# Cross-attention and mixture-of-experts layers: TensorE leaves out repeated semaphore waits, and value products wait once a batch

## The reference

```python
def _L0_xattn_ref(x, ctx, Wq, bq, Wkv, bkv, Wproj, bproj, gq, gk):
    q = (x @ Wq + bq).reshape(B, S, H, HD)
    q = rms_norm(q, gq).transpose(0, 2, 1, 3)
    kv = (ctx @ Wkv + bkv).reshape(B, Sc, 2, H, HD)
    k = rms_norm(kv[:, :, 0], gk).transpose(0, 2, 1, 3)
    v = kv[:, :, 1].transpose(0, 2, 1, 3)
    ...
    scores = jnp.einsum('bhsd,bhtd->bhst', q, k) * scale
    attn = jax.nn.softmax(scores, axis=-1)
    out = jnp.einsum('bhst,bhtd->bhsd', attn, v)
    ...
    return out @ Wproj + bproj
...
x = x + _L0_xattn_ref(_layernorm(x, axis=-1), ctx_1024, ...)
x = x + _L0_ffn_ref(_layernorm(x, axis=-1), ...)      # quantized, conv, SiLU
x = x + _L1_xattn_ref(_layernorm(x, axis=-1), ctx_1024, ...)
x = x + _L1_ffn_ref(_layernorm(x, axis=-1), ...)      # softmax gate, 8 experts, SiLU(g) * u
```

## Time and profile before

| | |
|---|---|
| time, median of 3 runs | 1279.05 us (1277.93 to 1282.09) |
| the profiled execution's own time | 1278.19 us |
| its span, first to last instruction | 1276.3 us |
| busy: PE, PEld | 1156.3 us (91%), 833.9 us (65%) |
| busy: DVE, ACT, POOL | 1044.5 (82%), 865.6 (68%), 699.2 (55%) |
| mean granted TensorE clock | 0.951 |

### The profile page before, as it was taken

The page is one execution under the profiler, slowest core; times in us unless marked ns, Lnnn a source line. Parts: engine busy times, 40 slices in busy tenths (PEclk is TensorE's granted clock), DMA queues, the critical chain, the costliest instruction groups (busy, mean ns, idle before and its releaser), DMA issues.

```text
span 1276.3 us, 27899 instructions
## 1 busy us (share of the span) xinstructions
PE 1156.3 (91%) x10338; PEld 833.9 (65%) x10338; DVE 1044.5 (82%) x2837; ACT 865.6 (68%) x1684; POOL 699.2 (55%) x827
## 2 busy tenths in 40 slices
PE   1567578999999999999999999999999998999998
PEld 1344445675767677676767676776757676766775
DVE  3667877989889898989899898989898898768653
ACT  0335455786868686777868676877868685866665
POOL 3202122666464757566574747566664647455775
PEclk9656879999999999999999999999999999999999
DMA  6000001001010101001010101001010101000000
GB/s 198 21 10 12 12 25 29 17 4 43 10 37 17 38 17 37 18 5 43 10 36 18 37 17 37 18 21 33 4 44 9 38 2 37 17 10 17 10 9 9
DMA packets 63847, 32.69 MB, mean 26 GB/s; under 512 B 29281, under 2 KB 63073, under 8 KB 63329
## 3 DMA queue, kind: packets, MB, share of 16 engines
q1 hardware_dynamic: 61696, 26.83, 8.4%
q10 hardware_dynamic: 2016, 4.08, 0.9%
HBM read 24.73 MB, written 4.19 MB: 23 GB/s over the span
## 4 chain that ended last, share of the span: by engine, by line
PE 78%; DVE 10%; POOL 6%; ACT 3%; issue 2%; DMA 1%; SPq 0%; POOLq 0%; DVEq 0%; ACTq 0%
PE py L697 16%; PE pa L543 5%; PE pa L508 4%; PE pg L687 3%; PE pu L687 3%; PE pg L688 3%; PE pg L689 3%; PE pu L688 3%; PE pu L689 3%; PE pa L532 3%; POOL xn L856 2%; PE pa L550 2%; PE pb L590 2%; PE pb L596 2%; PE pa L697 2%
## 5 line engine op out<-in xcount | busy, mean ns | idle before, releaser
L895 POOL TENSOR_TENSOR moe<-moe 128x512 f32<-128x512 f32 x256 | 331.1, 1295 | 293.3 <-DVE moe L1194 179.0
L697 PE MATMUL py<-wd_s,moe 128*128 128x128 f32 x1856 | 250.7, 280 | 0.2
L697 PEld LDWEIGHTS py<-wd_s,moe 128*128 128x128 f32 x1856 | 232.9, 192 | 19.9 <-issue 4.4
L1073 DVE TENSOR_REDUCE q_st<-pa 128x4 f16<-128x480 f32 x256 | 168.4, 658 | 42.1 <-PE pa L508 40.2
L1194 DVE SCALAR_TENSOR_TENSOR moe<-tg,pg 128x512 f32<-128x512 f32 x232 | 157.8, 680 | 49.0 <-ACT tg L818 46.7
L818 ACT ACTIVATE tg<-pg 128x512 f32<-128x512 f32 x232 | 140.2, 604 | 75.2 <-PE pg L689 74.3
L756 ACT ACTIVATE probs<-pa 120x512 f32<-120x512 f32 x256 | 138.9, 598 | 49.4 <-PE pa L532 46.9
L832 ACT ACTIVATE moe<-pu 128x512 f32<-128x512 f32 x232 | 139.2, 600 | 15.9 <-PE pu L689 13.9
L508 PE MATMUL pa<-kbd,qkht 128*128 128x480 f16 x256 | 101.3, 396 | 24.5 <-DVE q_st L1073 19.5
L856 POOL TENSOR_SCALAR xn<-x,lnm,lnr 128x128 f32<-128x128 f32 x192 | 90.0, 481 | 5.2
L687 PE MATMUL pg<-x4h,wg_h 128*128 128x512 f16 x232 | 88.9, 383 | 3.7 <-DVE moe L1194 0.2
(11 more groups left out here) (200 smaller groups left out, 2743.8 us busy)
## 6 DMA issues: line engine op xcount, KB each, us to landing
xin<-in_x SPq DMA_DIRECT2D x16, 256.0 KB, 2.8
xres<-in_x SPq DMA_DIRECT2D x16, 256.0 KB, 3.0
kbd<-qkht SPq DMA_DIRECT2D x256, 7.5 KB
out_x<-acc SPq DMA_DIRECT2D x16, 256.0 KB, 4.2
ctxt_a<-in_ctx_t SPq DMA_DIRECT2D x16, 240.0 KB, 2.7
ctxt_b<-in_ctx_t SPq DMA_DIRECT2D x16, 240.0 KB, 3.4
ctxn_b<-in_ctx SPq DMA_DIRECT2D x16, 240.0 KB, 4.1
wd_s<-in_wd ACTq DMA_DIRECT2D x1, 1024.0 KB, 8.4
```

Of the source, the lines that this page charges most:

```text
L697: mm = pe.matmul(moe_y(g, e)[:, j, :], hu[:, u % 3, j * S:(j + 1) * S], wd_s[:, u, :], start=(half == 0 and j == 0), stop=(half == 1), ski ...
L895: pool.tensor_tensor(hu[:, u % 3, :], gw[:, u % 3, :], us[:, u % 3, :], ALU.mult)\
L1073: dve.tensor_reduce(q_st[:, t, 4 * c:4 * c + 4, 3 * HD], pa[:, BM, 0:4 * SC].rearrange("p (h k) -> p h k", h=4), AX.X, ALU.max, negate=Tru ...
```

## The change

TensorE keeps, while the program is built, the highest value of each semaphore that it has waited for (`passed`). A wait for no more than that is left out (`need`); all waits of TensorE but the very first go through it, those of `take` too. `scores` takes S1 before S0. `values` waits once, for the fourth exponential of its batch, instead of once before each group of four products. No product, no order and no other engine changes.

```diff
+            passed = {}
+
+            def need(signal, value):
+
+                if passed.get(signal, 0) < value:
+                    passed[signal] = value
+                    pe.wait_ge(signal.sem, value)
+
             held = {}
 
             def take(psum, done, g, k=1):
 
                 if psum in held:
-                    sem, value = held[psum]
-                    pe.wait_ge(sem, value)
-                held[psum] = (done.sem, done.at(g, k))
+                    need(*held[psum])
+                held[psum] = (done, done.at(g, k))
...
                 elif name == "stacks":
                     if t == 0:
-                        pe.wait_ge(dup_done.sem, dup_done.at(g, 2))
-                        pe.wait_ge(ql_done.sem, ql_done.at(g))
-                        pe.wait_ge(kl_done.sem, kl_done.at(g))
-                    pe.wait_ge(max_done.sem, max_done.at(g, 4 * t + 4))
+                        need(dup_done, dup_done.at(g, 2))
+                        need(ql_done, ql_done.at(g))
+                        need(kl_done, kl_done.at(g))
+                    need(max_done, max_done.at(g, 4 * t + 4))
                     take(BM, st_done, g, t + 1)
...
                     if c == 0:
-                        pe.wait_ge(st_done.sem, st_done.at(g, t + 1))
+                        need(st_done, st_done.at(g, t + 1))
+                    take(S1, p_done, g, 4 * t + 2 * c + 2)
                     take(S0, p_done, g, 4 * t + 2 * c + 1)
-                    take(S1, p_done, g, 4 * t + 2 * c + 2)
...
                 elif name == "values" and c == 1:
                     if t == 0:
-                        pe.wait_ge(v_done.sem, v_done.at(g))
+                        need(v_done, v_done.at(g))
                     take(BO, o_done, g, t + 1)
+                    need(p_done, p_done.at(g, 4 * t + HQ))
                     for i in range(HQ):
-                        pe.wait_ge(p_done.sem, p_done.at(g, 4 * t + i + 1))
                         for n in range(NQ):
...
                 elif name == "hit":
-                    pe.wait_ge(hr_done.sem, hr_done.at(g, t + 1))
+                    need(hr_done, hr_done.at(g, t + 1))
                     take(PB, hit_done, g, t + 1)
```

More of the change, by code:

```diff
@@ L463, in do_n @@
                 if step == "xn1t":
-                    pe.wait_ge(xn1_done.sem, xn1_done.at(g))
+                    need(xn1_done, xn1_done.at(g))
                     take(BANK["xn1t"], xn1t_done, g)
@@ L469, in do_n @@
                 elif step == "qkv":
-                    pe.wait_ge(xn1t_done.sem, xn1t_done.at(g))
+                    need(xn1t_done, xn1t_done.at(g))
                     take(BANK["q"], qb_done, g)
@@ L475, in do_n @@
                     mm.then_inc(q_ps.sem, 1)
-                    pe.wait_ge(ctxa_in.sem, ctxa_in.at(g, 16))
+                    need(ctxa_in, ctxa_in.at(g, 16))
                     take(BANK["k"], kb_done, g)
@@ L488, in do_n @@
                     qkh = bank("qkht").bitcast(F16)
-                    pe.wait_ge(q_hi_done.sem, q_hi_done.at(g))
+                    need(q_hi_done, q_hi_done.at(g))
                     take(BANK["qkht"], qkht_done, g)
@@ L492, in do_n @@
                         pe.transpose(qkh[:, j * S:(j + 1) * S], q_hi[:, j, :], id_h[:, :])
[L493 removed]
+                    need(kh_done, kh_done.at(g))
                     for j in range(GB):
@@ L503, in do_a @@
                     if t == 0:
-                        pe.wait_ge(kbd_in[c].sem, kbd_in[c].at(g, 16 * HQ))
+                        need(kbd_in[c], kbd_in[c].at(g, 16 * HQ))
                         if c == 0:
-                            pe.wait_ge(qkht_done.sem, qkht_done.at(g))
+                            need(qkht_done, qkht_done.at(g))
                     take(BM, max_done, g, 4 * t + c + 1)
@@ L552, in do_a @@
                 elif name == "ont":
-                    pe.wait_ge(on_done.sem, on_done.at(g, GB))
+                    need(on_done, on_done.at(g, GB))
                     take(BM, ont_done, g)
@@ L558, in do_a @@
                 elif name == "proj":
-                    pe.wait_ge(ont_done.sem, ont_done.at(g))
+                    need(ont_done, ont_done.at(g))
                     if g == 0:
-                        pe.wait_ge(rest_in.sem, 16 * 12)
+                        need(rest_in, 16 * 12)
                     take(BO, x1_done, g)
@@ L570, in do_b @@
                 if name == "xit":
-                    pe.wait_ge(xq_done.sem, xq_done.at(g))
+                    need(xq_done, xq_done.at(g))
                     take(PB, xl_done, g)
@@ L577, in do_b @@
                     if t == 0:
-                        pe.wait_ge(xh_done.sem, xh_done.at(g))
+                        need(xh_done, xh_done.at(g))
                         if g == 0:
-                            pe.wait_ge(wint_done.sem, 1)
+                            need(wint_done, 1)
                     take(PB, cv_done, g, t + 1)
@@ L586, in do_b @@
                     if t == 0:
-                        pe.wait_ge(h2_done.sem, h2_done.at(g, KB))
+                        need(h2_done, h2_done.at(g, KB))
                     take(PB, hr_done, g, t + 1)
@@ L598, in do_b @@
                 elif name == "fc2":
-                    pe.wait_ge(hit_done.sem, hit_done.at(g, GB))
+                    need(hit_done, hit_done.at(g, GB))
                     take(PB, x2_done, g)
@@ L612, in do_d @@
                 if step == "xn3t":
-                    pe.wait_ge(xn3_done.sem, xn3_done.at(g))
+                    need(xn3_done, xn3_done.at(g))
                 elif step == "bf":
-                    pe.wait_ge(xn3t_done.sem, xn3t_done.at(g))
+                    need(xn3t_done, xn3t_done.at(g))
                 elif step == "s1":
-                    pe.wait_ge(bf_done.sem, bf_done.at(g))
-                    pe.wait_ge(ctxb_in.sem, ctxb_in.at(g, 32))
+                    need(bf_done, bf_done.at(g))
+                    need(ctxb_in, ctxb_in.at(g, 32))
                 elif step == "p1t":
-                    pe.wait_ge(p1n_done.sem, p1n_done.at(g))
+                    need(p1n_done, p1n_done.at(g))
                 elif step == "oc":
-                    pe.wait_ge(p1t_done.sem, p1t_done.at(g))
+                    need(p1t_done, p1t_done.at(g))
                 elif step == "fused":
-                    pe.wait_ge(oc_done.sem, oc_done.at(g))
+                    need(oc_done, oc_done.at(g))
                 elif step == "xn4t":
-                    pe.wait_ge(xn4_done.sem, xn4_done.at(g))
+                    need(xn4_done, xn4_done.at(g))
                 elif step == "gate":
-                    pe.wait_ge(x4l_done.sem, x4l_done.at(g))
+                    need(x4l_done, x4l_done.at(g))
                     if g == 0:
-                        pe.wait_ge(w_lo.sem, 3)
+                        need(w_lo, 3)
                 if step in d_read:
```

5 lines of the change are left out of this document (2 added, 3 removed).

## The result

The changed kernel takes 1288.75 us (median of 6 runs, 1286.31 to 1291.78) beside 1278.88 for the kernel before (6 runs, 1277.56 to 1282.09): a ratio of 1.0070, 95% interval 1.0059 to 1.0080. It is slower by about 9 us. (The ratio sets runs against runs; the quotient of the two medians is 1.0077.) Its profiled execution took 1287.36 us, 1285.5 of it the span, 9.2 more than the span before. All lines of the change stand 7 further down: the max products are L515 now, the stack transposes L525, the score products L539, the value products L550, the transposes of xq L581, the exponentials L763.

What follows compares the result with a forecast made beforehand. TensorE was taken as the bound, busy 69.4 of 71 us per period. Joined-wait delays of 4.2 and 5.0 less gains of 1.0 and 0.3 made +7.9 us, forecasting 1286.5 us, range 1279.5 to 1291.

Steps and rivals of the forecast that it cites:

- the likeliest case: Whole kernel: slower by more than the 3.8 us that a measurement tells from no change; chance 0.71.
- Part 2, repeating part: 217 to about 1063 us: joined wait delays value products at two places in each of twelve periods, +4.2 us.
- Part 2, fill: 40 to 217 us: joined wait makes value products start later, +5.0 us, between +2.5 and +6.1.
- Part 1: Waits left out: 0 in the repeating part, -1.0 us in the fill, -0.3 us in the drain.
- the 27 waits: Fill: held standalone waits that become carried, 0.08 us each; about 13 on the chain give -1.0 us.
- The clock: Rival: shifted start spares slow-clock stretches from 1063 us or in the fill, -3.5 us, giving 1283; favourable side 0.10.
- The queue as the limit: Rival: each standalone wait takes 51 ns from TensorE, 410 fewer save 20.9 us, giving 1258; 0.09 with its weaker form.
- The absorbing period: Rival: periods absorb the joined wait's delay, only fill and drain count, +3.7 us, giving 1282.7; chance 0.16.

Runs made afterwards that it cites:

- e2_merge_alone: Kernel before, with only the value products' joined wait for the fourth exponential added, all other waits kept: 1291.42 us, ratio 1.0082 to before.
- e12_merge_late: Changed kernel, with the joined wait only from group 3 on and one wait per exponential in the fill: 1282.75 us, ratio 1.0022 to before.
- e3_carried: Changed kernel, with the joined wait placed first in the source so the weight load carries it: 1286.79 us, ratio 1.0059 to before.
- e11: Changed kernel, with the joined wait only in groups 0 to 2 and one wait per exponential afterwards: 1285.70 us, ratio 1.0044 to before.
- e1_no_merge: Changed kernel, with value products again waiting for each exponential in turn; left-out waits stay out: 1278.59 us, ratio 0.9988 to before.
- e4_idle_waits: Kernel before, with 768 pairs of already satisfied waits (one carried, one standalone) between down products: 1279.15 us, ratio 0.9998 to before.
- e5_short_waits: Kernel before, with 768 pairs of already satisfied waits (one carried, one standalone) between short value products: 1289.35 us, ratio 1.0087 to before.
- e6_two_waits: Changed kernel, but a batch waits for the third exponential and its last four products for the fourth: 1279.81 us, ratio 1.0012 to before.
- e7_order: Changed kernel with one wait per exponential, and each product group's last-arriving wait placed first in the source: 1275.96 us, ratio 0.9979 to before.
- e10_short_carried: Kernel before, with 768 single satisfied waits between short value products, each carried by a weight load: 1279.91 us, ratio 0.9998 to before.
- e8_shift50: Kernel before, with a gate product in group 3 repeated 50 times, 10.8 us more TensorE work: 1289.24 us, ratio 1.0085 to before.

## Why the prediction was right, and where its terms were off

1286.5 us was forecast and 1288.75 measured, inside the range, and slower as the likeliest case had it; the mechanism is the forecast one.

- *Part 2, repeating part.* Forecast 12 x 0.35 = 4.2 us, measured 5.06 in the changed kernel, 5.04 in e2_merge_alone, 5.23 in e12_merge_late. Nothing absorbs it, as argued. The term is 0.07 a period too small, and the price of the held wait is all of it: I took 0.11 us from the exponential's end to the product, and it is 0.14 and 0.15 at the two places. With the 0.05 us of e3_carried at both, the same sum gives 0.23 a period, and its twelve take 855.35 - 852.58 = 2.77 us, 0.23 each. The 0.03 that I took off because a value product starts with its load is not to be taken off.
- *Part 2, fill.* Forecast +5.0 (2.5 to 6.1), measured 5.5 to 5.9 by traces and 7.1 (about 5 to 9) by the medians, which would make it the term that was sized worst. The total hides that single batches came out otherwise. Between e11 and e12 the delay grows by 0.28, 0.40 and 0.83 us at the batches of 56.6, 66.73 and 76.47 (forecast 0.1, 0.36, 0.78). At the ends of the batches of 85.88 and 116.75 it grows by 0.74 and 0.72 (forecast 1.35, 1.33), but by 0.94 more until the one of 131.6, which I had counted at nothing with a bound of 1.1; 0.53 of it is made good by 176.88. Then come 0.83 at 188.45 (forecast 0.78), 0.44 at 199.15 (not counted), and 0.82 at 210.8 where I gave 0.3. The clock has a part in this: from 85.2 to 88.6 us e11 has a granted clock of 1.00 and e12 of 0.50. Between the kernel before and the changed one, which are nearer to each other there (0.73 and 0.83), the batch of 85.88 adds 1.15 us. That the delay of 131.6 is the earlier one handed on by VectorE's chain is argued, not tested.
- *Part 1.* Forecast -1.0, and -0.3 in the drain; e1_no_merge shows -1.5 (-2.7 to -0.4) in the times; its trace does not show at which of the 27 waits. That the score products gain nothing in the repeating part, that the max products' 7.0 us stay, and that what the stack transposes gain is lost at xq, are all in the waits shown above. A held wait is 0.095 us cheaper when it is carried (e3_carried), for the 0.08 that I took.
- *The clock.* It stood in a rival at 0.10, not in the sum, and it came true beside the forecast: 2.4 us back after 1080 us. I had read 3.5 us off the clock of 0.95 in that stretch, taking TensorE as the limit all through it; the half clock lay on 7 us in which TensorE had stood idle just before, and that prices it at 2.4.
- *The sum, mended*: 5.1 + 5.5 (or 7.1) - 1.5 - 2.4 = 6.7 to 8.3 us, beside a measured 0.70%, 9.0 us (7.5 to 10.2). The forecast of 7.9 came from terms too small in the delays and without the clock's gain; the two errors nearly cancelled, so that its closeness is in part luck. In the two traces the 9.2 us between the spans divide so: 0.84 at the first value product, before the joined wait has cost anything, 5.70 from there to the first xq transpose of the repeating part, 5.06 in the periods, and -2.38 by the clock. Two runs of different kernels differ by as much as the first of these without a cause that the traces show, and part 1's gain is hidden in it.
- *The rivals.* The queue as the limit is excluded for this change by e1_no_merge and e4_idle_waits. But satisfied waits can cost: e5_short_waits loses 11.1 us. The prediction had no row for such waits between short products. In e5 they cost 0.019 us each, in e4 nothing that can be told. The absorbing period is excluded by e12_merge_late. What it is worth to hand off each exponential by itself is shown by e1_no_merge against the changed kernel: one wait for each gives back 1.0070 - 0.9988 = 0.82%.

Still open: why single runs of one kernel spend more or less of the fill at a granted clock of 0.50, and so how much of the fill's 5.5 to 7.1 us is waiting and how much the slower clock after it. No run held the clock fixed.

## What to carry to other kernels

A wait that was joined with later ones cost here the time by which the first consumer started late, at both places of a period (0.42 us together, where TensorE is busy 69 of 71 us) and in the fill (5.5 to 7.1 us); look for the batches that start before their last producer ends, and join only the hand-offs that are done by then (e6_two_waits: three of four were free in the periods here, and cost about 3 us in the fill, where some batches start before the third has ended). Satisfied standalone waits cost nothing that can be told between down products (e4_idle_waits), and 0.02 us each between value products, which start 33 ns apart on average (e5_short_waits). Where a group waits for several things, put the one that comes last where the weight load carries it (0.05 us from the exponential to the product in e3_carried, for 0.14 to 0.15), and then ask who waits next: in the twelve periods of e7_order VectorE took the whole gain back (852.76 us, for 852.57 in e1_no_merge).

## What was not expected of the hardware

- A satisfied standalone wait is shown with 51 ns in every trace, but costs TensorE nothing that can be told between down products (e4_idle_waits) and 0.019 us between value products (e5_short_waits); 768 more carried ones cost nothing there (e10_short_carried).
- From the end of an exponential to the matmul it is 0.14 to 0.15 us through a standalone wait (changed kernel) and 0.05 through the weight load's own (e3_carried).
- The same 2.4 us of idle time of TensorE (2.40 to 2.48 in the traces), after more than 840 us at a granted clock of 1.00, comes with 6.8 us at 0.50 in the kernel before (1080.0 to 1086.8), in e1, e4, e6 and e10, with 3.4 us in e3 (1090.4 to 1093.8), e11 and e12, and with none in the changed kernel, e2, e5, e7 and e8; e8, e11 and e12 have 3.4 us more some 65 us later (1156.9, 1153.6 and 1152.5). The order of TensorE's work there is one and the same (e8 has its 50 products far ahead of it); its start had moved, later or earlier. A kernel whose TensorE gets 10.8 us more to do (e8_shift50) can lose a half-clock stretch by it.
